# Moving the 32-column matmuls of a grouped convolution to other places in TensorE's program

## What is computed

```python
enh = conv(conv(x, w_conv1_pw, b_conv1_pw, 0), w_conv1_dw, b_conv1_dw, 1, groups=128)   # 1x1, then 3x3 depthwise
h = conv(x, w_conv2_g, b_conv2_g, 1, groups=16)                                         # 3x3 grouped, 16 outputs
h1, h2 = split(h, 2)
attn = conv(h1 * h2, w_conv2_pw, b_conv2_pw, 0) * attgamma + conv(x, w_conv211, b_conv211, 0)
attk = einsum('bpn,nm->bpm', attn, selfw)       # per pixel: a 2x2x9 kernel for each of 64 channel pairs
y = einsum('bpgij,bpgj->bpgi', attk, patches3x3(enh)) + einsum('bpn,nc->bpc', attn, selfb)
out = y * ga1 + enh + x
```

## Time and profile before

| | |
|---|---|
| median of 3 runs | 5361.32 us (5360.32 to 5362.08) |
| the profiled execution | 5362.06 us |
| its span, first to last instruction | 5360.3 us |
| mean granted clock of TensorE over the span | 0.995 of full speed |
| TensorE busy (matmuls) | 5267.2 us, 98% |
| VectorE busy | 5032.0 us, 94% |
| GpSimd busy | 4373.8 us, 82% |
| ScalarE busy | 3322.0 us, 62% |

### The profile page before, as it was taken

The page is one execution under the profiler, slowest core; times in us unless marked ns, Lnnn a source line. Parts: engine busy times, 40 slices in busy tenths (PEclk is TensorE's granted clock), DMA queues, the critical chain, the costliest instruction groups (busy, mean ns, idle before and its releaser), DMA issues.

```text
span 5360.3 us, 113060 instructions
## 1 busy us (share of the span) xinstructions
PE 5267.2 (98%) x37904; PEld 3936.0 (73%) x37904; DVE 5032.0 (94%) x5360; ACT 3322.0 (62%) x4094; POOL 4373.8 (82%) x2022
## 2 busy tenths in 40 slices
PE   8999999999999889999999999999999999999998
PEld 7888888888888657676776767676767677767676
DVE  7888888888888789999999999999999999999999
ACT  6888888888888555555555555555555555555552
POOL 4565656555565499999999999999999999999996
PEclk9999999999999989999999999999999999999999
DMA  3222222222222122222222222222222222222221
GB/s 93 77 72 75 74 75 74 73 75 70 78 71 78 61 84 88 72 86 73 85 74 83 77 80 79 78 81 75 84 74 86 72 87 70 87 72 87 72 87 44
DMA packets 175615, 413.21 MB, mean 77 GB/s; under 512 B 37200, under 2 KB 58768, under 8 KB 175504
## 3 DMA queue, kind: packets, MB, share of 16 engines
q1 hardware_dynamic: 175568, 412.59, 25.1%
HBM read 228.94 MB, written 145.77 MB: 70 GB/s over the span
## 4 chain that ended last, share of the span: by engine, by line
PE 60%; ACT 2%; DVE 2%; issue 1%; POOL 0%; ACTq 0%; DVEq 0%; POOLq 0%
PE ps_t L1077 23%; PE ps_k L1057 19%; PE ps_m L1038 10%; PE ps_m L1014 5%; PE ps_t L1089 2%; ACT tap L1196 1%; PE ps_m L1045 1%; PE ps_t L1087 1%; DVE products L1281 1%; ACT out_sb L1176 1%; POOL enh L971 0%; DVE ps_k L1281 0%; DVE basis L360 0%; DVE products L347 0%; DVE products L1287 0%
## 5 line engine op out<-in xcount | busy, mean ns | idle before, releaser
L971 POOL TENSOR_TENSOR enh<-enh,tap 128x1024 f32<-128x1024 f32 x1024 | 2261.3, 2208 | 162.9 <-ACT tap L1196 119.6
L1281 DVE TENSOR_TENSOR products<-ps_k,enh 128x1024 f32<-128x1024 f32 x1728 | 2049.5, 1214 | 21.1 <-PE ps_k L1057 16.4
L1057 PE MATMUL ps_k<-att,basis 128*128 128x512 f32 x4608 | 1640.4, 450 | 15.9 <-DVE products L1281 11.1
L504 POOL TENSOR_TENSOR hidden_lo<-hidden,hidden_hi 128x1024 fp32r<-128x1024 f32 x256 | 693.5, 2729 | 718.7 <-DVE hidden_hi L709 718.7
L1196 ACT ACTIVATE tap<-e,dw 128x1024 f32<-128x1024 f32 x1024 | 1139.6, 1144 | 204.2 <-POOL enh L971 202.7
L1057 PEld LDWEIGHTS ps_k<-att,basis 128*128 128x128 f32 x4608 | 744.7, 190 | 502.2 <-issue 156.3
L977 POOL TENSOR_TENSOR products<-products 128x1024 f32<-128x1024 f32 x448 | 1073.6, 2396 | 29.3 <-DVE products L1281 29.3
L1077 PE MATMUL ps_t<-ident,products 128*128 128x128 f32 x5120 | 720.8, 274 | 17.6 <-ACT out_sb L1176 17.2
L1287 DVE TENSOR_TENSOR products<-ps_k,products 128x1024 f32<-128x1024 f32 x576 | 704.6, 1223 | 17.7
L1281 DVE TENSOR_TENSOR ps_k<-ps_k,enh 128x1024 f32<-128x1024 f32 x576 | 704.7, 1223 | 15.0 <-PE ps_k L1057 14.8
L1077 PE MATMUL ps_t<-ident_swap,products 128*128 128x128 f32 x5120 | 715.0, 272 | 0.0
(11 more groups left out here) (118 smaller groups left out, 7125.3 us busy)
## 6 DMA issues: line engine op xcount, KB each, us to landing
xin<-layer_out SPq DMA_DIRECT2D x64, 1280.0 KB, 7.3
xt<-in_x SPq DMA_DIRECT2D x128, 512.0 KB, 4.1
layer_out<-xo SPq DMA_DIRECT2D x128, 512.0 KB, 2.9
x_own<-layer_out SPq DMA_DIRECT2D x128, 512.0 KB, 3.9
out<-out_sb SPq DMA_DIRECT2D x256, 256.0 KB, 2.1
att<-att_hi SPq DMA_DIRECT2D x512, 32.0 KB, 2.2
att<-att_lo SPq DMA_DIRECT2D x512, 32.0 KB, 2.0
enh<-edge_rows SPq DMA_DIRECT2D x64, 130.0 KB, 2.1
```

Of the source, the lines that this page charges most:

```text
L504: nc.gpsimd.tensor_tensor(hidden_lo[:, h, :, :], hidden[:, h, :, :], hidden_hi[:, h, :, :].bitcast(FP32), ALU.subtract).then_inc(hidden_lo ...
L971: nc.gpsimd.tensor_tensor(own, own, tap_sb[add % TAP_BUFFERS][:, 0:hi - lo, :], ALU.add).then_inc(dw_done, 1)
L1057: mm = nc.tensor.matmul(ps_k[NEXT_ORDER[KERNEL_BUFFER[q]] if p else KERNEL_BUFFER[q]][:, BANK * s:BANK * (s + 1)], basis[:, 2 * t + s, :], ...
L1281: nc.vector.tensor_tensor(out, kernels, enh[p][:, r:r + CHUNK_ROWS, dx:dx + W].unsqueeze(1).to_broadcast([C, 2, CHUNK_ROWS, W]), ALU.mult) ...
```

## The change

It is a change of the table `CONV_SLOTS` alone. All nine taps of a band are still done by the same 36 matmuls in the same order.

```diff
-CONV_SLOTS = [24, 24, 26, 26, 26, 26, 33, 33, 33, 33, 36, 36, 41, 41, 41, 41, 45, 45]
+CONV_SLOTS = [25, 25, 25, 25, 25, 25, 33, 33, 33, 33, 39, 39, 39, 39, 45, 45, 45, 45]
```

## The result

| | before | changed |
|---|---|---|
| median | 5360.82 us (5359.98 to 5362.08, 4 runs) | 5417.3 us (5416.49 to 5418.65, 4 runs) |
| the profiled execution | 5362.06 us | 5416.49 us |
| its span | 5360.3 us | 5414.8 us |

The ratio is 1.0105, with a 95% interval from 1.0093 to 1.0117. The change is 56.5 us slower by the medians; the forecast was 5411 us, slower, with a range from 5385 to 5436.

The account below looks back on a forecast made before the run. VectorE was taken to lose time only where a burst of TensorE work precedes a pair needed soon. Slot 45's 41.0 us plus slot 25's 7.4, added to 5362.1, gave 5411 us, range 5385 to 5436.

Parts of the forecast that it names:

- What bounds the kernel: Both engines nearly full; TensorE holds VectorE up at products 6, 25 and 30, 0.56 us a step.
- Slot 45, 0.65 us a step: Second tap between K3 and K6 adds 0.86, 0.21 comes back; product 6 0.65 us later, 63 times: 41.0 us.
- Slot 25, 0.12 us a step: Three taps ahead of K24: product 24 later by 0.37, less 0.25 of old delays; 62 steps: 7.4 us.
- The time: Whole kernel: 48.4 us more than the profiled execution's 5362.1, forecast as 5411 us.
- The old delays at 25 and 30 go: K25 follows K24 without a place, so delays at products 25 and 30 vanish (0.15 + 0.10 us).
- Slots 33 to 41 at nothing: Taps of slots 36 and 41 moved to 39, ahead of K35, needed last in the band: no cost.
- `conv_done` at nothing: ScalarE's wait for the last tap, the h2 DMAs and `h_prod` all move back by 0.65 us: no cost.
- TensorE's total sets the pace: Rival: only TensorE's sum counts, two place surcharges fewer, 0.68 us a step; floor 5327 us; chance 6%.
- the weight loads' waits are slack: Rival: TensorE can take in the taps of slots 45 and 25, nothing changes: 5361 us; chance 5%.
- slot 25 is covered: Rival: slot 45 costs, slot 25's three taps do not; 0.40 us a step, 5387 us; chance 10%.
- the h2 rows come late: Rival: moved `conv_done` delays the DMAs, VectorE stands at `h_prod` in slot 8; further 0.5 us a step, 5442; chance 4%.
- The signs: Expected in the profile: product 6 waits 0.96 us, step 54.6 us, TensorE's busy time falls, more waits ahead of K1 and K34.

Follow-up runs that it names:

- the run with slots 38 and 39: Kernel before, with slot 24's tap moved to 26, slot 36's to 38 and slot 41's two to 39 (five places): 5341.66 us against 5359.66.
- The run with slot 46: Kernel before, with one tap moved from slot 41 to slot 46, between K4 and K5 (seven places): 5472.95 us against 5361.53.
- the run with four places: Kernel before, with taps regrouped as three in slot 26, two in 33, three in 39, one in 45: 5347.26 us against 5361.53.

## Why the prediction was right, point by point

- **What bounds the kernel.** Right, and the base of all else: VectorE's lateness against its own rhythm, 0.55 us a step, was the measure, not the 98% of TensorE or the waits of its weight loads.
- **Slot 45, 0.65 us a step.** Right in each piece. The place took 1.87 us, K1 waited for merge 33, and product 6 came 0.96 us late. The run with slot 45 alone gave 41.8 us for a term of 41.0.
- **Slot 25, 0.12 us a step.** Right in its mechanism, mis-sized: it measured 0.26 in the changed kernel (0.49 at product 24, less 0.23). The step that failed is the start of product 24 at "about 3023.59", 0.04 us behind the end of K24. That is the distance at product 6. In the changed kernel product 24 starts 0.13 behind K24's end (3040.06 to 3040.19), which is 0.09 us more in 62 steps, 6 us. The rows of the kernel before held a warning. K25 ended at 3023.70 + 0.66 = 3024.36. Products 24 to 26 ended at 3023.14 + 3.71 = 3026.85; product 26 started 1.21 before that and product 25 1.13 earlier still, at 3024.51, so 0.15 behind its pair. The stretch from K22 to K24's end took 0.94 + 0.25 + 0.44 + 2.74 + 0.66 = 5.03 us instead of the 5.00 of the forecast, and the old delays were 0.23 instead of 0.25. These three make up the 0.14.
- **The time.** The forecast added 48.4 us, and the medians differ by 56.5. The 8 us that lack lie in slot 25 (0.14 x 62 = 9). That 5411 is only 6 us off is a little luck: the sum was added to a profiled execution that is 1.2 us above the median.
- **The old delays at 25 and 30 go.** Right, 0.14 + 0.09 against the 0.25 I had counted.
- **Slots 33 to 41 at nothing.** Right: all waits of VectorE are at products 6 and 24, and the run with slots 38 and 39 gained nothing clear of noise by them.
- **`conv_done` at nothing.** Right for this change: the distance between the two operations of VectorE around `h_prod` is 1.79 us before and after, so `h_prod` was not late. The run with slot 46 shows how near its end the cover is.
- **The rivals.** That TensorE's total sets the pace was shown wrong by the run with slot 45 alone and by the run with four places. The surcharge it rests on is real (25.6 us in the taps' own row). The Trainium skill's rule, in "TensorEngine Tiling (Array Packing)", section Key Properties, that a change of tiling mode drains the engine, agrees with that row and with the 0.28 us of a place that nothing covers; no run shows a drain apart from other costs of such a change. The rule does not say which change of mode lies on the path. That the weight loads' waits are slack was shown wrong by product 6, 0.96 us late. That slot 25 is covered was wrong by a fair margin: product 24 is 0.49 late. That the h2 rows come late was wrong too, as `h_prod` shows.
- **The signs.** The step came to 54.70 us, where 54.6 was named, and the waits ahead of K1 and K34 are there. TensorE's busy time fell, but by 1.6 us only.

## What to carry to other kernels

When two in-order engines are both nearly full, ask for each move which consumer stands next behind it and how late that consumer already is; the busy shares and the total saved told nothing here. In this kernel, batching work to save a fixed cost per batch paid when the batch went behind the piece that was needed next (16.9 us less), and lost when it went ahead of it (9.0 us more), with the same three taps on the two sides of K24. The last instruction of a batch has waiters of its own on other engines, and their cover should be measured, not assumed.

## What the runs showed of the hardware

Four matmuls of 32 output columns into the four quarters of a bank start within 0.02 us of one another in the changed kernel's place of slot 25, and the next four follow 0.43 us later. So they take together 0.43 us for each of their two float32 MATMULs, and a tap 0.86 or 0.87. Going from full-width matmuls to these and back costs 0.34 or 0.35 us in the chain, whether one, two or three taps stand between (1.01, 1.87 and 2.74 us).

The distance from the end of a pair to the product that waited for it depends on the product. Over all traces it is 0.04 us at products 6, 16, 18 and 23, in the runs in which they wait, and 0.12 or 0.13 at 5, 14, 15, 24, 25 and 30. The traces hold a difference that fits. In the instructions of 6, 16, 18 and 23 the wait for the pair's semaphore is their own. The others wait for a second semaphore (`place_free`), and ahead of them VectorE's sequencer has an instruction of its own (L151) that waits for the pair: for product 24 it starts at 3040.10, 0.04 us behind K24's end, and the product 0.09 us later. No run changes the waits, so this cause is not shown.

The step alternates between two lengths from band to band, 53.72 and 53.87 us before and 54.63 and 54.78 with the change, with the same order of instructions on TensorE. The prediction had seen this at product 25. Its cause was not followed up.
